# One shared PSUM bank for the small pieces of a graph-network kernel, and a new order of the tasks on every engine

## The chip, the cores and the metric

The kernel runs on one core of one Trainium2 chip. The metric is the device time of one execution in microseconds (us). The core's five engines work from queues of their own and meet only at semaphores: PE is TensorE (matmuls, with PEld for its weight loads), DVE is VectorE, ACT is ScalarE, POOL is GpSimd, and SP is SyncE, which only issues DMAs here. An instruction stands in its engine's queue in program order, so one that waits holds up all that stands behind it.

## The reference, cut to what matters

There are 32 graphs of 256 nodes with 64 features. For each node j of a graph the layer sums, over its neighbours k (the mask is set for about 5 of 256 nodes, itself included), a ReLU of a hidden vector of 192 values, and projects the sum back to 64:

```python
mask = (adj > 0.0).astype(x.dtype)
xj_proj = x @ W1a
diff = x[:, :, None, :] - x[:, None, :, :]
h = relu(xj_proj[:, :, None, :] + diff @ W1b + b1)
hm = einsum('bjkh,bjk->bjh', h, mask)
deg = sum(mask, axis=-1)
out = layernorm(x + hm @ W2 + deg[..., None] * b2)
```

The hidden vector of a pair (j, k) is u(j) + v(k) with u = x (W1a + W1b) + b1 and v = -x W1b. It is needed only where the mask is set.

## The kernel before, in words

**Two graphs at a time.** The 32 graphs make 16 pairs. A pair has TILES = 4 tiles of 128 nodes. The 192 hidden rows are split in a "main" part (128 rows, 4 groups of 128 columns) and a "tail" part (64 rows of each graph, put together in 2 groups).

**Slots and pieces.** The nodes are sorted by their number of neighbours (`sort_key`, `keys`, `ranks`, `permutation`), and each neighbour of a node gets a slot. Slot s is needed only for the first CAPS[s] nodes of the order. There are eleven pieces: 0, 1 and 2 cover all 128 nodes; pieces 3 to 9 cover 118, 96, 72, 48, 28, 16 and 10 nodes; piece 10 is the "small" piece, six slots of 6 nodes. For each piece `select` (DVE) makes a 0/1 matrix `hot` out of the slot numbers `slotT`, `seed` (ACT) copies u into a PSUM bank, `gather` (PE) adds hot times v on top of it (v in two float16 halves, `vh` and `vl`), and `add` (DVE, line 1737) takes the ReLU and adds it to `sums`. Main piece 0 goes another way: `take_out` (ACT) and `add_taken` (POOL, line 685). The small piece is clamped by `clamp_small` (ACT, line 897), reduced by `reduce_small` (DVE) and added by `add_small`, which ends the pair's sums (semaphore `summed`).

**Units and banks.** Pieces are grouped in units; a unit is one bank's worth, seeded and gathered together. Two ring buffers of two banks each serve all of it: one half of a buffer for tail units, the other for main units, so a unit can be seeded only when the unit two before it has been added (`released`).

**Stages of a pair.** `masks`, `count_masks`, `count_least`, `count_rest` (DVE) count neighbours; `turn_masks`, `number_slots` (PE) with `copy_maskT`, `copy_slots` (ACT) make the slots; `sort_x`, `excess_tail`, `hidden_u_main`, `hidden_u_tail`, `hidden_v` (PE) with `copy_xs`, `copy_u_main`, `copy_u_tail`, `high_v`, `full_v` (ACT) and `low_v` (POOL) make u and v; `start_sums` (DVE, line 1681, once a pair) starts `sums`; then come the pieces; `project` (PE) waits for `summed`, `copy_y`, `unsort_y`, `add_residual` (DVE, sets `z_added`), `statistics` (DVE), the moments, `scale` (POOL) and the store end the pair.

**Order.** Nothing schedules at run time. Each engine has a prologue written out by hand, a `body(pair)` that is run for 13 pairs by `run` (a hardware loop over six of them) and mixes the work of three to five neighbouring pairs, and an epilogue written out by hand.

**Scaling of the inputs.** Before the first v can be computed the weights are scaled by a power of two: `first_max` and `first_scales` do it for pair 0 from its own x. For all other pairs `sum_chunk` (ACT) sums the absolute values of the whole x in four chunks (`x_all`), `most`, `spread_x` and `scales` make the second factor.

## Time and profile before

| | before |
|---|---|
| median of 3 runs (lowest to highest) | 253.78 us (253.54 to 254.46) |
| span of the profiled execution, first to last instruction | 253.0 us |
| PE busy, share of the span | 239.2 us, 95% |
| DVE busy | 230.0 us, 91% |
| ACT busy | 214.8 us, 85% |
| POOL busy | 133.1 us, 53% |
| instructions PE, DVE, ACT, POOL | 2813, 810, 636, 288 |

The median stands 0.8 us above the profiled span; the profiled execution has no other time on record. A matmul's record is longer than its turn on the engine: in a run of equal matmuls the starts are closer together than the durations, so a busy PE says little about how much PE has to spare, and the distance from start to start is read instead. DVE's and ACT's records overlap their neighbours a little in the same way.

In rows of the view by windows the columns are: the window, its length, then busy us and count of PE, PEld, DVE, ACT and POOL, the granted PE clock (1.00 is full), the DMA share and GB/s. In rows of the view by groups they are: line, engine, operation, output<-inputs, shape, count, busy us, mean ns of one, and idle time of the engine before it. In rows of the timeline: start, duration, engine, line, operation, operands and how many were put together in the row.

### The profile page before, as it was taken

How to read it: one execution, taken by the hardware profiler on the slowest of the kernel's cores; microseconds unless marked ns; L12 is line 12 of the kernel's file. 1: busy time of each engine (PE TensorE's matmuls, PEld its weight loads, DVE VectorE, ACT ScalarE, POOL GpSimd, SP SyncE). 2: the span in 40 equal slices, each digit the busy share in tenths (PEclk: the TensorE clock that was granted, in tenths of full speed). 3: DMA queues.
4: the chain of work that ended last, by engine and by line, in shares of the span. 5: the costliest groups of instructions: out<-in, count | busy, mean ns of one | idle time of the engine just before them, and what ended most of it. 6: DMA issues, size and time to landing. Idle time of an engine off the chain costs nothing. (4 is left out here: it accounts for less than half of the span.)

```text
span 253.0 us, 9425 instructions
## 1 busy us (share of the span) xinstructions
PE 239.2 (95%) x2813; PEld 190.5 (75%) x2813; DVE 230.0 (91%) x810; ACT 214.8 (85%) x636; POOL 133.1 (53%) x288
## 2 busy tenths in 40 slices
PE   7968999999999999999999999999999999999990
PEld 2536687878887978878877878878887879777870
DVE  4797799999999999999999999999999999979853
ACT  2396999898989999898989989898989898988820
POOL 1415252565555574655554564655655555454834
PEclk9997999999999999999999999999999999999997
DMA  6992003501312203031212203031310110000001
GB/s 196 349 352 87 1 3 127 146 4 43 106 45 51 98 22 106 26 106 41 105 41 76 69 20 99 27 105 44 104 45 25 41 29 17 4 21 3 25 21 51
DMA packets 10552, 18.21 MB, mean 72 GB/s; under 512 B 1296, under 2 KB 7696, under 8 KB 10512
## 3 DMA queue, kind: packets, MB, share of 16 engines
q1 hardware_dynamic: 10512, 17.73, 21.7%
q8 instruction: 19, 0.31, 0.5%
q14 instruction: 21, 0.17, 0.2%
HBM read 15.63 MB, written 2.10 MB: 70 GB/s over the span
## 5 line engine op out<-in xcount | busy, mean ns | idle before, releaser
L1287 PE MATMUL ring<-hot,vh 128*128 128x128 bf16 (+9 forms) x768 | 115.8, 254 | 0.9 <-ACT ring L869 0.4
L1287 PE MATMUL ring<-hot,vl 128*128 128x128 bf16 (+9 forms) x768 | 113.9, 251 | 0.0
L1737 DVE SCALAR_TENSOR_TENSOR sums<-ring,sums 128x256 f32<-128x256 f32 (+14 forms) x304 | 104.9, 375 | 8.7 <-PE ring L1287 4.0
L1287 PEld LDWEIGHTS ring<-hot,vh 128*128 128x128 f16 (+1 forms) x768 | 61.0, 102 | 18.9 <-issue 7.9
L874 ACT COPY ring<-u_sb 128x144 f32<-128x144 f32 (+13 forms) x256 | 65.2, 302 | 9.6 <-DVE sums L1737 7.9
L1287 PEld LDWEIGHTS ring<-hot,vl 128*128 128x128 f16 (+1 forms) x768 | 62.2, 103 | 2.8
L631 POOL TENSOR_TENSOR vl<-vf,vh 128x384 f16<-128x384 f32 x32 | 34.4, 1075 | 49.2 <-ACT vf L839 32.3
L869 ACT COPY ring<-u_sb 128x512 f32<-128x512 f32 (+1 forms) x80 | 45.0, 565 | 0.9 <-PE ring L1111 0.4
L1710 DVE TENSOR_SCALAR hot<-slotT 128x944 bf16<-128x944 f16 (+6 forms) x112 | 28.5, 267 | 0.0
L685 POOL TENSOR_TENSOR sums<-taken,sums 128x512 f32<-128x512 f32 x16 | 20.3, 1272 | 11.7 <-ACT taken L891 11.7
L790 ACT CAST maskT<-bx 128x512 bf16<-128x512 f32 x32 | 18.4, 583 | 8.8 <-PE bx L1139 7.7
L797 ACT CAST slotT<-bx 128x512 f16<-128x512 f32 x32 | 19.0, 596 | 1.3 <-PE bx L1156 1.3
L1530 DVE TENSOR_REDUCE counts<-mask 128x8 f32<-128x1024 bf16 x16 | 19.1, 1195 | 0.0
L1257 PE MATMUL bx<-w2ms,sums 128*128 128x64 f32 x128 | 18.6, 268 | 0.0
L602 POOL TENSOR_TENSOR step<-stats 128x4 f32<-128x4 f32 x16 | 7.1, 441 | 21.1 <-DVE stats L1771 21.1
L839 ACT COPY vf<-bx 128x384 f32<-128x384 f32 x32 | 15.2, 477 | 3.5 <-PE bx L1225 3.4
L1257 PEld LDWEIGHTS bx<-w2ms,sums 128*128 128x128 f32 x128 | 16.9, 192 | 0.2
L1269 PE MATMUL bx<-y_sb,permT 128*128 128x64 f32 x128 | 16.2, 269 | 0.0
L832 ACT CAST vh<-bx 128x384 f16<-128x384 f32 x32 | 15.6, 487 | 0.3 <-PE bx L1225 0.3
L1269 PEld LDWEIGHTS bx<-y_sb,permT 128*128 128x128 f32 x128 | 15.5, 191 | 0.3 <-ACT y_sb L853 0.2
L1681 DVE SCALAR_TENSOR_TENSOR sums<-u_sb,bx 128x768 f32<-128x768 f32 x16 | 15.1, 945 | 0.1
L585 POOL TENSOR_TENSOR excess<-deg,given 128x4 bf16<-128x4 f32 x16 | 3.2, 203 | 22.0 <-DVE given L1606 22.0
(117 smaller groups left out, 470.8 us busy)
## 6 DMA issues: line engine op xcount, KB each, us to landing
adj_sb<-adj SPq DMA_DIRECT2D x16, 512.0 KB, 3.5
x_sb<-x_pairs SPq DMA_DIRECT2D x16, 128.0 KB, 2.3
xT_sb<-xT SPq DMA_DIRECT2D x16, 128.0 KB, 2.4
x_all<-x SPq DMA_DIRECT2D x4, 512.0 KB, 8.1
out<-o_sb SPq DMA_DIRECT2D x16, 128.0 KB, 1.7
wts<-weights SPq DMA_DIRECT2D x1, 417.0 KB, 4.8
cst_general<-general SPq DMA_DIRECT2D x1, 256.0 KB, 2.7
cst_half<-half SPq DMA_DIRECT2D x1, 137.0 KB, 3.2
```

The source lines that it names most:

```text
L631: eng.tensor_tensor(vl[pair.side][:, c, :], vf[:, c, :], vh[pair.side][:, c, :], ALU.subtract).then_inc(vl_ready, 1)
L685: eng.tensor_tensor(to, taken[piece][:, :, :], to, ALU.add).then_inc(taken_added, 1)
L790: eng.copy(maskT[:, g * NT:g * NT + NT, :].rearrange("p t r -> p (t r)"), (bx1, bx2)[g][:, :]).then_inc(maskT_copied, 1)
L797: eng.copy(slotT[:, g * NT:g * NT + NT, :].rearrange("p t r -> p (t r)"), (bx0, bx1)[g][:, :]).then_inc(slots_copied, 1)
L869: last = eng.copy(to, u.unsqueeze(1).broadcast_to([P, sum(map(whole, pieces)), n, P]))
L874: last = eng.copy(view(pair, part, unit, piece), v if slots == 1 else v.unsqueeze(3).broadcast_to([P, n, cap, slots]))
L1257: eng.matmul(to[:, g * O:g * O + O], sums[pair.side][:, NT + g * NT + t, :], w2ms[scaled(pair)][:, :], start=(g == 0), stop=False, skip_gr ...
L1269: last = eng.matmul(bx3[:, at:at + O], permT[pair.side][:, g * NT + t, :], y_sb[:, t * 2 + g, :], start=True, stop=True)
L1287: return eng.matmul(to if part == "main" else to[g * HT:g * HT + HT], values, selection, start=False, stop=final, skip_group_check=True)
L1530: eng.tensor_reduce(counts[pair.side][:, :, :].rearrange("p g c -> p (g c)"), mask[pair.side][:, :, :].rearrange("p c (k n) -> p (c k) n", ...
L1710: eng.tensor_scalar(to[:, :, :, off:off + n], slots, float(MARK + s), None, ALU.is_equal).then_inc(hot_ready, 1)
L1737: eng.scalar_tensor_tensor(out=to, in0=view(pair, part, unit, piece), scalar=0.0, in1=to, op0=ALU.max, op1=ALU.add).then_inc(added[part], 1)
```

## The change

Three things change. First, pieces are grouped in other units: piece 7 moves to the unit of piece 4, and the last unit is now pieces 8, 9 and 10 in both parts. Second, that last unit is "joint": its 6 groups x 62 columns of main and tail lie in one bank of the main half, seeded by one `seed_joint` for both parts, clamped by one `clamp_small`, and added by `add_joint` over all 6 groups; the tail half of the ring then turns over 3 units a pair and not 4. Third, the tasks stand in another order on all engines, and some gathers, `project` and `unsort_y` can be issued in parts (`first`, `end`) with other work between them. The load of pair 2's x also waits for `first_max` now.

```diff
-UNITS = {"tail": [[0, 1], [2, 3], [4, 5, 6], [7, 8, 9, 10]], "main": [[0], [1], [2], [3], [4], [5, 6], [7, 8, 9, 10]]}
+UNITS = {"tail": [[0, 1], [2, 3], [4, 7, 5, 6], [8, 9, 10]], "main": [[0], [1], [2], [3], [4, 7], [5, 6], [8, 9, 10]]}
...
+JOINT = {part: NU[part] - 1 for part in PART}
+RING_UNITS = {"tail": NU["tail"] - 1, "main": NU["main"]}
...
+                if not pair.general and isinstance(pair.n, int) and pair.n == 2:
+                    eng.wait_ge(x_max0_ready, 1)
...
+            def seed_joint(pair):
+
+                eng.wait_ge(u_copied["main"], pair.n + 1)
+                eng.wait_ge(u_copied["tail"], pair.n + 1)
+                released(pair, "main", JOINT["main"] - BUFFERS)
+                for piece in UNITS["main"][JOINT["main"]]:
+                    _, _, cap, slots = PIECES[piece]
+                    v = u_sb[pair.side][:, :, 0:cap]
+                    last = eng.copy(joint_view(pair, piece),
+                                    v if slots == 1 else v.unsqueeze(3).broadcast_to([P, GROUPS, cap, slots]))
+                last.then_inc(seeded["main"], 1)
...
-            def clamp_small(pair, part):
-                eng.wait_ge(gathered[part], NU[part] * (pair.n + 1))
+            def clamp_small(pair):
+                for part in PART:
+                    eng.wait_ge(gathered[part], NU[part] * (pair.n + 1))
...
+            def add_joint(pair, piece):
+
+                nth = JOINT_ADDS.index(piece)
+                if nth:
+                    eng.wait_ge(joint_added, len(JOINT_ADDS) * pair.n + nth)
+                else:
+                    for part in PART:
+                        eng.wait_ge(gathered[part], NU[part] * (pair.n + 1))
+                        eng.wait_ge(added[part], ADDS[part] * (pair.n + 1))
+                    eng.wait_ge(clamped, pair.n + 1)
+                to = sums[pair.side][:, :, 0:PIECES[piece][2]]
+                eng.scalar_tensor_tensor(out=to, in0=joint_view(pair, piece), scalar=0.0, in1=to,
+                                         op0=ALU.max, op1=ALU.add).then_inc(joint_added, 1)
```

A piece of DVE's new body; the other engines' orders are rewritten in the same way:

```diff
             def body(pair, has=always):
...
                 if has(-3):
+                    add_residual(elder)
+                if has(0):
+                    ranks(pair)
+                if has(-2):
+                    add(older, "main", 3)
+                if has(0):
+                    ranks_above(pair)
+                    permutation(pair)
+                if has(-1):
+                    start_sums(old)
```

**Where instructions move.** First VectorE's prologue, from the scaling of the first weights on. Before, the selection matrices of pair 0 follow it at once:

```order
L1650 TENSOR_SCALAR w1abs<-w1ab,up_bits 128x256
L1651 TENSOR_SCALAR w1vs<-wts,up_bits 128x192
L1698 TENSOR_SCALAR hot<-slotT 128x512 x2
L1522 TENSOR_SCALAR mask<-adj_sb 128x1024
L1610 CAST ident<-cst_half 128x128
L1701 TENSOR_TENSOR hot<-slotT,cst_half 128x512
L1530 TENSOR_REDUCE counts<-mask 128x8
```

The change has this ahead of the scaling (its lines have other numbers):

```order
L1675 SCALAR_TENSOR_TENSOR w_abs<-wts 64x192
L1583 TENSOR_SCALAR mask<-adj_sb 128x1024
L1591 TENSOR_REDUCE counts<-mask 128x8
L1667 TENSOR_REDUCE given<-above 128x4
L1607 TENSOR_TENSOR least<-counts,cst_single 128x8
L1689 TENSOR_REDUCE x_max<-x_sb 128x1
L1680 TENSOR_REDUCE w_top<-ring 128x1
```

and this from the last weight scaling on:

```order
L1712 TENSOR_SCALAR w1vs<-wts,up_bits 128x192
L1583 TENSOR_SCALAR mask<-adj_sb 128x1024
L1759 TENSOR_SCALAR hot<-slotT 128x512 x2
L1762 TENSOR_TENSOR hot<-slotT,cst_half 128x512
L1685 TENSOR_REDUCE x_most<-x_sum 128x1
L1771 TENSOR_SCALAR hot<-slotT 128x944
```

The mask and the counts of pair 1 moved ahead of the scaling, and the mask of pair 2 (the second `mask` row, right behind `w1vs`) moved ahead of pair 0's first selection matrix; the search of the largest x sum (`x_most`) moved into pair 0's selections.

Second, VectorE in the body, the end of a pair's adds, before (L1737 are the adds of single parts):

```order
L1737 SCALAR_TENSOR_TENSOR sums<-ring,sums 128x2x28
L1530 TENSOR_REDUCE counts<-mask 128x8
L1737 SCALAR_TENSOR_TENSOR sums<-ring,sums 128x2x16
L1737 SCALAR_TENSOR_TENSOR sums<-ring,sums 128x4x28
L1737 SCALAR_TENSOR_TENSOR sums<-ring,sums 128x2x10
L1737 SCALAR_TENSOR_TENSOR sums<-ring,sums 128x4x16
L1745 TENSOR_REDUCE small_sum<-small 128x36
L1737 SCALAR_TENSOR_TENSOR sums<-ring,sums 128x4x10
```

and of the change (L1810 is `add_joint`):

```order
L1796 SCALAR_TENSOR_TENSOR sums<-ring,sums 128x4x48
L1591 TENSOR_REDUCE counts<-mask 128x8
L1810 SCALAR_TENSOR_TENSOR sums<-ring,sums 128x6x16
L1796 SCALAR_TENSOR_TENSOR sums<-ring,sums 128x256
L1817 TENSOR_REDUCE small_sum<-small 128x36
L1810 SCALAR_TENSOR_TENSOR sums<-ring,sums 128x6x10
```

Four small adds (2x16, 4x16, 2x10, 4x10 columns) became two over six groups, and the adds of piece 7 (2x28, 4x28) moved up to those of piece 4.

Third, TensorE in its prologue around `spread_x` (the fp32 matmul from `x_most`), before:

```order
L1225 MATMUL bx<-w1vs,xT_sb 128x192 x4
L1111 MATMUL ring<-ones 128x512 x2
L1123 MATMUL bx<-reaches,cst_order 128x64 x3
L1139 MATMUL bx<-perm,mask 128x128 x8
L1100 MATMUL ring<-ident,x_most 128x128
```

and of the change:

```order
L1244 MATMUL bx<-xs,w1abs 128x256
L1132 MATMUL ring<-ident,x_most 128x128
L1257 MATMUL bx<-w1vs,xT_sb 128x192 x4
L1143 MATMUL ring<-ones 128x512 x2
L1155 MATMUL bx<-reaches,cst_order 128x64 x3
L1171 MATMUL bx<-perm,mask 128x128 x4
```

`spread_x` moved ahead of pair 0's `hidden_v` (the w1vs rows), so that v of pair 0 now stands behind a matmul that needs the sums over all of x.

## Rows read from the trace of the kernel before

**Rows 1.** The page's first part, busy time of the engines.

```profile
PE 239.2 (95%) x2813; PEld 190.5 (75%) x2813; DVE 230.0 (91%) x810; ACT 214.8 (85%) x636; POOL 133.1 (53%) x288
```

**Rows 2.** Windows cut at starts of start_sums of pairs 0, 1, 4, 8, 12, 15.

```profile
0.00:33.63 33.63, 27.56 (x224) 16.92 (x225) 25.05 (x79) 22.30 (x53) 10.64 (x24) 0.95 0.54 185
...
75.41:131.89 56.48, 56.02 (x693) 45.81 (x692) 55.07 (x197) 52.23 (x156) 32.94 (x69) 1.00 0.21 67
...
188.32:229.67 41.35, 40.90 (x510) 33.89 (x509) 38.28 (x137) 38.33 (x116) 22.75 (x50) 1.00 0.07 22
```

**Rows 3.** Timeline of TensorE, first and last row of one pair's turn.

```profile
119.97 0.39 PE L1237 MATMUL bx<-ident,perm 128*128 128x128 bf16 x4
...
134.10 0.39 PE L1237 MATMUL bx<-ident,perm 128*128 128x128 bf16 x4
```

**Rows 4.** Waits of VectorE and ScalarE: us in total, times, longest.

```profile
DVE sums L1737 <- PE ring L1287: 4.0, 13, 0.9
DVE sums L1737 <- POOL sums L685: 2.7, 2, 1.5
...
ACT ring L874 <- DVE sums L1737: 7.9, 19, 0.7
```

**Rows 5.** Groups by line and shape: VectorE's small adds.

```profile
L1737 DVE SCALAR_TENSOR_TENSOR sums<-ring,sums 128x96 f32<-128x96 f32 x16 | 4.1, 257 | 0.1
L1737 DVE SCALAR_TENSOR_TENSOR sums<-ring,sums 128x64 f32<-128x64 f32 x16 | 3.6, 224 | 0.0
L1737 DVE SCALAR_TENSOR_TENSOR sums<-ring,sums 128x40 f32<-128x40 f32 x16 | 3.1, 191 | 0.0
L1737 DVE SCALAR_TENSOR_TENSOR sums<-ring,sums 128x32 f32<-128x32 f32 x16 | 2.9, 181 | 0.1
L1737 DVE SCALAR_TENSOR_TENSOR sums<-ring,sums 128x20 f32<-128x20 f32 x16 | 2.7, 168 | 0.0
```

**Rows 6.** The load of pair 2's adjacency: its issue and time to landing.

```profile
L486 SPq DMA_DIRECT2D adj_sb<-adj x1: 652/652/652, 8.2 to 8.2; - x1
...
DMA to landing us min/median/max: 9.1/9.1/9.1
```

**Rows 7.** Timeline of VectorE in the prologue.

```profile
12.40 0.49 DVE L1698 TENSOR_SCALAR hot<-slotT 128x512 bf16<-128x512 f16 x2
12.81 0.69 DVE L1522 TENSOR_SCALAR mask<-adj_sb 128x1024 bf16<-128x1024 f32 x1
...
16.49 0.95 DVE L1681 SCALAR_TENSOR_TENSOR sums<-u_sb,bx 128x768 f32<-128x768 f32 x1
...
18.11 0.69 DVE L1589 TENSOR_TENSOR perm<-cst_half,rank 128x512 f32<-128x512 f16 x1
...
21.43 0.29 DVE L1659 TENSOR_REDUCE x_top<-ring 128x1 f32<-128x128 f32 x1 [0.65 <-PE ring L1100]
...
22.50 1.21 DVE L1530 TENSOR_REDUCE counts<-mask 128x8 f32<-128x1024 bf16 x1
...
33.63 0.95 DVE L1681 SCALAR_TENSOR_TENSOR sums<-u_sb,bx 128x768 f32<-128x768 f32 x1
```

**Rows 8.** A window behind TensorE's stops in the prologue.

```profile
21.20:24.20 3.00, 3.00 (x31) 2.72 (x31) 2.21 (x8) 1.31 (x3) 1.87 (x5) 0.50 0.53 183
```

**Rows 9.** Timelines of VectorE and TensorE at the last pair's end.

```profile
243.49 0.18 DVE L1753 TENSOR_TENSOR sums<-sums,small_sum 128x36 f32<-128x36 f32 x1
...
242.59 1.67 PE L1326 MATMUL bx<-ones 128*128 128x512 bf16 x7
244.10 0.55 PE L1257 MATMUL bx<-w2ms,sums 128*128 128x64 f32 x4
```

**Rows 10.** One source line each: durations in ns, min/median/max.

```profile
L1698 DVE TENSOR_SCALAR hot<-slotT x32: 279/285/741, 12.4 to 220.9; 128x512 bf16<-128x512 f16 x32
...
L631 POOL TENSOR_TENSOR vl<-vf,vh x32: 912/920/1357, 16.9 to 230.4; 128x384 f16<-128x384 f32 x32
```

More of the change, by code:

```diff
@@ new lines, in project, with unsort_y @@
+                if end == 3 * NT:
+                    last.then_inc(y_ready, 1)
+            def unsort_y(pair, first=0, end=TILES):
+                if first == 0:
+                    eng.wait_ge(y_copied, pair.n + 1)
+                    eng.wait_ge(permT_copied, pair.n + 1)
+                for c in range(first, end):
+                    g, t = divmod(c, NT)
+                    last = eng.matmul(bx3[:, (TILES + c) * O:(TILES + c + 1) * O], permT[pair.side][:, c, :],
+                                      y_sb[:, t * 2 + g, :], start=True, stop=True)
+                if end == TILES:
+                    last.then_inc(z_ready, 1)
@@ L1368, in body @@
                 if has(1):
-                    gather(new, "main", 4)
+                    gather(new, "main", 3, 2, 4)
                 if has(2):
@@ L1372, in body @@
                 if has(1):
-                    gather(new, "main", 5)
+                    gather(new, "tail", 2)
+                    gather(new, "main", 4, 0, 2)
                 if has(3):
@@ L1922, in _ @@
             run(eng, body)
+            select(Pair(0, 13), 6)
+            sort_key(Pair(0, 14))
+            add(Pair(0, 12), "main", 2)
+            add_residual(Pair(0, 11))
+            ranks(Pair(0, 14))
+            add(Pair(0, 12), "main", 3)
+            ranks_above(Pair(0, 14))
+            permutation(Pair(0, 14))
+            start_sums(Pair(0, 13))
+            add(Pair(0, 12), "tail", 4)
+            add(Pair(0, 12), "main", 4)
+            add(Pair(0, 12), "main", 7)
+            select(Pair(0, 13), 7)
```

792 lines of the change are left out of this document (398 added, 394 removed).

## The prediction

> **What bounds the kernel now.** I read the busy shares first. TensorE is at 95% and VectorE at 91% of the span [rows 1], but a matmul's record is longer than its turn, so the 95% doesn't say that TensorE is full. Next I cut the span at the starts of `start_sums`, which comes once a pair. The eight middle pairs take 14.12 us each (56.48 over four), the last three before the end 13.78, and the head up to the start of pair 1's sums 33.63 us [rows 2]. From there to pair 15's start at 229.67 are fourteen turns of 14.00 us on average. In a middle turn VectorE is busy for 55.07 / 4 = 13.77 us, so it idles for 0.35 us. ScalarE is busy for 13.06 and GpSimd for 8.2 us.
>
> For TensorE I read the starts: one turn goes from 119.97 to 134.10 [rows 3]. Between its first and last row I count a dozen places where the next start is later than the last form's own spacing; together these are about 1.06 us, so its own work is about 14.13 - 1.06 = 13.07 us. About seven of them, near 0.09 us each, stand where full-width matmuls follow half-width ones or the reverse, with every input long there. I take these 0.6 us as TensorE's own, which makes its line 13.65 to 13.7 us. Two engines within 0.5 us of the whole turn thus hold each other up. The list of waits says the same: VectorE's adds wait for gathers 13 times (4.0 us), the seeds wait for adds 19 times (7.9 us) [rows 4]. A gain has to shorten both lines, or take out waits between them.
>
> **What the change is worth in a middle turn.** *VectorE.* The adds of 32, 64, 20 and 40 columns take 181 + 224 + 168 + 191 = 764 ns. They become one of 96 columns (257 ns) and one of 60, which lies between 40 and 64 columns, 191 to 224; I take 215 ns [rows 5]. Records overlap their neighbours by about 80 ns, so two instructions fewer give back 2 x 80 less: 764 - 472 - 160 = 0.13 us a turn. VectorE can then turn in 13.77 - 0.13 = 13.64 us. *ScalarE* loses three copies and a clamp; it is busy for only 13.06 of 14.12 us [rows 2], so I cost this at nothing. If a seed were always late, this could give at most the 7.9 us that seeds wait now [rows 4], which are mostly its own idle time. *TensorE* keeps its 96 gather matmuls and their columns. In the new order the tail units stand together with `sort_x`, and I count five changes of width instead of seven, which is 0.18 us less: 13.5 us.
>
> So neither engine can turn in less than 13.5 to 13.65 us. Do the waits go? I laid the new bodies beside each other, with starts from the trace. The chain that comes nearest to closing starts at `project`: its product gives y, z, then `add_residual`; behind that VectorE has ranks, main 3, permutation, `start_sums`, tail 4, main 4 and main 7; then comes `seed_joint`, and only then main unit 6 on TensorE. The joint seed needs both adds of main 4 and 7 out of the bank. From `project` to main unit 6 this chain takes about as long as TensorE itself needs (9.25 us by my count from the starts), and 4.5 us more bring TensorE back to `project`: 13.75 us. I take 13.75 us, 0.37 less than 14.12. Twelve full turns and two shorter ones at the end (0.1 each) give 4.6; I allow 0.5 for turns before the new order has settled: **-4.1 us**. The bounds are the engine lines themselves, (14.00 - 13.5) x 14 = -7 us, and on the other side 0.15 us more waiting in each turn than now, +2 us.
>
> **The head.** Here I expect a loss. VectorE began pair 0's selections at 12.40 [rows 7]. Now the mask of pair 2 stands in front of them. Its adjacency was issued at 8.2 and landed 9.1 us later, at 17.3 [rows 6], and nothing in the change brings it sooner, since the loads ahead of it are the same. The mask's 0.6 us follow: the first selection at 18.0 instead of 12.40. Queued behind it are all selections of pair 0, `x_most`, and through that `spread_x`, behind which TensorE now has pair 0's `hidden_v`. From the first selection to `start_sums` were 4.1 us, with a mask of 0.6 and a count of 1.1 that are now done earlier: 2.4 remain. In front of `start_sums` come now also the second scaling (21.43 to 22.50, and its wait of 0.65 for TensorE) and pair 1's ranks and permutation, which stood behind it (from 17.36, where `start_sums` let go, to 18.7) [rows 7]: 1.7 + 1.3. Sum: 23.4 instead of 16.49.
>
> Most of this comes back, since the order ahead is then shorter. From the count at 22.50 to pair 1's `start_sums` at 33.63 were 11.13 us [rows 7], with waits of 0.9 and 1.5 in them [rows 4] and main 4 of 0.5 that now comes later: 8.2 us of work. In the new order that count stands about 1.5 us behind pair 0's `start_sums`, at 24.9. In front of the selections of pair 1 I expect a stop of about 1.9 us, since slot numbers need `turn_masks`, which stands behind `turn_perm`, which waits for `start_sums`; then two mask copies and four other copies are ahead of the second `copy_slots`. That puts pair 1's `start_sums` at 24.9 + 8.2 + 1.9 = 35.0. Add 0.8 for TensorE: after the stops in the old head the granted clock was 0.50, the 1.2 GHz level, from 21.20 to 24.20 [rows 8], and the new head lets TensorE idle longer (about 2 us up to `spread_x`, more up to pair 1's masks). 35.8 against 33.63: **+2.2 us**. If the stop is hidden and the clock stays up it is nothing, and it is +4 if the half clock lasts through pair 1.
>
> The Trainium skill (TensorE: Matmul & The Clock Gate, "What's actually happening") says that the gate's throttled state is the default and that activity releases it. The trace agrees with it here, with 0.50 behind the stops and 1.00 in the middle turns.
>
> **The end.** From 229.67 to the last add at 243.49 VectorE's work falls by two pairs' 0.13 us. Seven filler matmuls ran from 242.59 and `project` started at 244.10, 0.61 us after the last add [rows 9]; they now stand before main unit 1 of pair 15, where they can delay its gathers by 1.5 us that TensorE can spare less. I take 0.4 for the earlier `project` and 0.2 for the adds: **-0.6 us**, between -1.2 and +1.
>
> **Sum.** -4.1 + 2.2 - 0.6 = -2.5 us; the profiled span of 253.0 becomes 250.5. The median lies 0.8 above the span, so I forecast 251.3 us.
>
> **The rivals.** *The body gains and the head loses* is the forecast; with a turn of 13.65 to 13.85 us it gives 249.5 to 252.5. Chance 0.42.
>
> *The head costs nothing, or the turn gets near the engine lines.* For it: VectorE's wait for the adds taken out by GpSimd (2.7 us in two stops [rows 4]) lies in the head and in the end, and the new order has more work in front of main 1. The time is 251.3 - 2.2 = 249.1, or with a turn of 13.55 about 248.5. Chance 0.18.
>
> *VectorE's selections get shorter.* They take 279 ns at best and up to 741, and GpSimd's `low_v` 912 to 1357 [rows 10]: something holds both now and then. With two selections of this form in a turn, one slowed by 0.1 us, all of it is 0.1 x 14 = 1.4 us: 249.9, inside the first rival's time. Chance as a separate case 0.05. The Trainium skill (GPSIMD Engine Reference, "Key points") says that GpSimd shares its SBUF interfaces with VectorE, in contention with two-port modes and two SBUF inputs; the durations in rows 10 are of that kind, and no row shows the cause.
>
> *The joint bank is a new wait.* One seed now serves main and tail of the last unit. If main 4 and 7 are added 0.25 us later than I count, TensorE stops in front of main unit 6 in every turn, which turns in 14.0 us and more. At 14.12 nothing of the body's gain is left, and the head and end make it 253.8 + 2.2 - 0.6 = 255.4. It becomes slower than before by over 0.5% from a turn of about 14.1 on. For it: seeds already wait for adds 19 times. Against it: ScalarE has four instructions less. Chance 0.19.
>
> *No net change:* a turn near 13.95 loses to the head what the body gains; 252.6 to 254.9. Chance 0.16.
>
> **How the numbers follow.** About 0.5% (1.3 us) is what a measurement of this kernel can tell from no change. Faster than 252.5: most of the first case, both gains: 0.60. Within 0.5%: 0.19. Slower: 0.21. The range 248.3 to 255.0 leaves out the best and the worst corner, one in ten each; the likeliest case alone has 249.5 to 252.5.
>
> **What would show it.** In the trace after: pair 1's `start_sums` near 35.8 (the head is wrong below 34.5); VectorE idle just ahead of the mask at 17.3; middle turns of 13.65 to 13.85; no stop of TensorE over 0.1 us in front of the 124-column gathers; TensorE's clock at half somewhere between 19 and 27 us. The prediction is wrong if the middle turn is under 13.5, since then TensorE's width changes aren't its own time, or if pair 2's adjacency lands much before 17 us.

## The result and the profile after

The changed kernel takes 253.12 us (median of 16 runs, 252.27 to 254.37). The kernel before, run beside it, took 254.73 us (16 runs, 253.54 to 256.04); the ratio is 0.9938, with an interval of 0.9923 to 0.9954. So it is faster by 0.6%, about 1.6 us. I had forecast faster, by 2.5 us, to 251.3 us. In the whole study one execution was slow (one of run 2's ten, 300.87 us at a lower clock); no ratio contains it.

The busy shares of the page after the change, which stand against [rows 1]:

```profile
PE 235.9 (94%) x2810; PEld 188.7 (75%) x2813; DVE 226.6 (90%) x778; ACT 209.8 (84%) x572; POOL 121.4 (48%) x288
```

VectorE has 32 instructions fewer and ScalarE 64 fewer. Three windows answer to [rows 2]: the head up to pair 1's `start_sums`, four middle turns (pairs 4 to 8), and the end from pair 15's `start_sums`. The columns are length, then busy us (instructions) of PE, PEld, DVE, ACT, POOL, then clock, DMA share, GB/s.

```profile
0.00:36.72 36.72, 29.09 (x218) 17.13 (x219) 24.65 (x78) 22.05 (x50) 10.60 (x26) 0.86 0.49 170
77.95:132.49 54.54, 54.54 (x695) 45.36 (x692) 54.23 (x190) 50.88 (x142) 28.92 (x68) 1.00 0.23 69
...
227.03:250.90 23.87, 17.39 (x185) 13.49 (x183) 15.24 (x56) 11.05 (x35) 9.74 (x31) 0.97 0.06 20
```

Four turns now take 54.54 instead of 56.48 us, and TensorE and VectorE are busy for practically all of it. The head grew from 33.63 to 36.72, the end from 23.30 to 23.87. From pair 1 to pair 15 are (227.03 - 36.72) / 14 = 13.59 us a turn, against 14.00. In this pair of traces the change is therefore -5.7 us in the body, +3.1 in the head and +0.6 in the end, -2.1 together (253.0 to 250.9).

The timeline of VectorE in the new head, which stands against [rows 7]; the bracket is the idle time before a row and what ended it:

```profile
17.20 0.69 DVE L1583 TENSOR_SCALAR mask<-adj_sb 128x1024 bf16<-128x1024 f32 x1 [2.55 <-DMA adj_sb<-adj]
17.81 0.49 DVE L1759 TENSOR_SCALAR hot<-slotT 128x512 bf16<-128x512 f16 x2
...
23.77 0.94 DVE L1742 SCALAR_TENSOR_TENSOR sums<-u_sb,bx 128x768 f32<-128x768 f32 x1
```

The mask of pair 2 waits for its adjacency until 17.20, as forecast (17.3), the first selection starts at 17.81 instead of 12.40 (forecast 18.0), and `start_sums` at 23.77 (forecast 23.4). What lasts much longer than forecast is TensorE's half clock. These are four windows of the same trace, columns as above; the last but two is the granted clock, 0.50 being the 1.2 GHz level:

```profile
18.00:21.00 3.00, 2.25 (x10) 1.65 (x10) 2.56 (x15) 0.00 (x0) 0.00 (x0) 0.50 0.02 5
21.00:24.00 3.00, 1.50 (x9) 0.41 (x7) 2.05 (x11) 2.14 (x5) 1.47 (x2) 0.50 0.52 171
24.00:27.00 3.00, 2.75 (x24) 2.20 (x26) 2.83 (x6) 2.12 (x4) 3.00 (x9) 0.50 0.15 56
27.00:30.00 3.00, 3.00 (x44) 2.34 (x40) 0.89 (x4) 2.58 (x8) 0.66 (x2) 0.92 0.00 0
```

Before, only the stretch of [rows 8] was at 0.50. Now it is all of 18 to 27 (by narrower windows from about 17.2 to 27.5); between 15 and 18 TensorE was busy for 0.84 of 3 us.

The end, in rows of TensorE and then VectorE:

```profile
230.41 0.21 PE L1327 MATMUL ring<-hot,vh 128*128 128x124 bf16 x1 [1.05 <-ACT ring L914]
```

```profile
232.31 0.26 DVE L1810 SCALAR_TENSOR_TENSOR sums<-ring,sums 128x96 f32<-128x96 f32 x1 [1.55 <-ACT small L939]
...
242.63 0.19 DVE L1824 TENSOR_TENSOR sums<-sums,small_sum 128x36 f32<-128x36 f32 x1
```

From `start_sums` of pair 15 to the last add are now 15.60 us, against 229.67 to 243.49 = 13.82 in [rows 2, 9]. What follows the last add is shorter (8.3 instead of 9.5 us), since the filler no longer stands in front of `project` (run 3).

### The profile page after: what moved, and what is told of

It is laid out like the page before. It is cut to its first block and busy times, and to the rows that moved or that the text cites. A ratio compares the mean times of both kernels' runs of the same rounds, so it can differ in the third digit from the quotient of the medians.

```text
span 250.9 us, 9244 instructions
## 1 busy us (share of the span) xinstructions
PE 235.9 (94%) x2810; PEld 188.7 (75%) x2813; DVE 226.6 (90%) x778; ACT 209.8 (84%) x572; POOL 121.4 (48%) x288
## 5 line engine op out<-in xcount | busy, mean ns | idle before, releaser
L1327 PE MATMUL ring<-hot,vh 128*128 128x128 bf16 (+9 forms) x768 | 117.4, 255 | 1.3 <-ACT ring L914 1.0
L1327 PE MATMUL ring<-hot,vl 128*128 128x128 bf16 (+9 forms) x768 | 116.3, 251 | 0.0
L1796 DVE SCALAR_TENSOR_TENSOR sums<-ring,sums 128x256 f32<-128x256 f32 (+10 forms) x240 | 97.8, 428 | 4.3 <-PE ring L1327 1.9
L661 POOL TENSOR_TENSOR vl<-vf,vh 128x384 f16<-128x384 f32 x32 | 29.7, 929 | 63.2 <-ACT vf L870 59.4
L903 ACT COPY ring<-u_sb 128x192 f32<-128x192 f32 (+8 forms) x160 | 49.3, 359 | 7.4 <-DVE sums L1796 7.4
L900 ACT COPY ring<-u_sb 128x512 f32<-128x512 f32 (+1 forms) x80 | 43.3, 559 | 0.4 <-issue 0.2
L1304 PE MATMUL bx<-y_sb,permT 128*128 128x64 f32 x128 | 18.6, 272 | 0.0
L1188 PE MATMUL bx<-maskT,cst_half 128*128 128x128 bf16 x128 | 16.1, 221 | 0.1
L1583 DVE TENSOR_SCALAR mask<-adj_sb 128x1024 bf16<-128x1024 f32 x16 | 11.0, 688 | 5.4 <-DMA adj_sb<-adj 5.4
L1257 PE MATMUL bx<-w1vs,xT_sb 64*128 64x192 f32 x128 | 15.5, 362 | 0.3 <-ACT u_sb L855 0.3
```

The costliest lines, as they stand in the source:

```text
L661: eng.tensor_tensor(vl[pair.side][:, c, :], vf[:, c, :], vh[pair.side][:, c, :], ALU.subtract).then_inc(vl_ready, 1)
L900: last = eng.copy(to, u.unsqueeze(1).broadcast_to([P, sum(map(whole, pieces)), n, P]))
L903: last = eng.copy(view(pair, part, unit, piece), u[:, :, 0:PIECES[piece][2]])
L1304: last = eng.matmul(bx3[:, (TILES + c) * O:(TILES + c + 1) * O], permT[pair.side][:, c, :], y_sb[:, t * 2 + g, :], start=True, stop=True)
L1327: return eng.matmul(to if part == "main" else to[g * HT:g * HT + HT], values, selection, start=False, stop=final, skip_group_check=True)
L1796: eng.scalar_tensor_tensor(out=to, in0=view(pair, part, unit, piece), scalar=0.0, in1=to, op0=ALU.max, op1=ALU.add).then_inc(added[part], 1)
```

## The experiments

Head, turn and end below are read as above: the start of pair 1's `start_sums`, the mean turn from pair 1 to 15, and what follows pair 15's `start_sums`. A ratio is to the kernel before, run on the same chip. The kernels of runs 5, 6, 9, 10 and 13 to 18 leave a part of the work out, as each says; all of these but 10 are one execution each, so I compare their turns only. Four traces in which only the prologue or the end differs (after, 1, 2, 3) have turns of 13.58 to 13.59, so a difference of 0.02 us in one trace means nothing, and one of 0.05 does.

**1. The mask of pair 2 behind the scales.**

```
             first_scales()
-            masks(Pair(0, 2))
             select(Pair(0, 0), 0)
...
             scales()
+            masks(Pair(0, 2))
             count_rest(Pair(0, 1))
```

> The changed kernel with one row moved: the mask of pair 2 behind the second scaling instead of ahead of pair 0's selections. Theory 1 (the wait for pair 2's adjacency holds the head): the first selection starts when the slot numbers are there, near 15.9 us instead of 17.8, x_most follows at about 16.9 (the fourth chunk's sum), hidden_v at about 18.0 instead of 19.5, and pair 1's start_sums comes about 1.5 us earlier than 36.7. The time falls by 1.2 to 1.8 us against the changed kernel, ratio to the kernel before 0.988. Theory 2 (the sums over x stand ahead of u on ScalarE, and u is there only at 17.9, so the mask covers itself): the head ends where it did, within 0.4 us, ratio 0.993.

251.19 us, ratio 0.9864 (0.984 to 0.9887). The first selection starts at 15.71, now waiting for the slots and no longer for the adjacency; the head is 35.78, turn 13.58, end 23.86. The edit gives 0.9 us against the trace of after; against the mean head of after (below, 37.2) 1.4; by the two ratios, taken on two chips, 0.7%, 1.9 us. Theory 1 was right. The half clock did not go with the wait: it lasts from about 17.2 to 27.5 here too. This is the fastest version of the study that does all of the work.

**2. `spread_x` behind `hidden_v` as well.**

```
-            spread_x()
             hidden_v(Pair(0, 0))
+            spread_x()
```

> As the kernel with the late mask, and spread_x behind pair 0's hidden_v instead of ahead of it. Theory 1: hidden_v then waits for u alone (17.9 us); since x_most is there at about 17 anyway, this gives 0 to 0.5 us more than the late mask alone. Theory 2 (TensorE's slow clock after its stops prices the head, not the stops themselves): hidden_v keeps its 1.6 us at the half clock, and pair 1's start_sums moves by less than 0.3 us against the late mask alone.

255.61 us, ratio 1.002 (1.0004 to 1.0035). The head is 40.48, 4.7 us more than in run 1. `hidden_v` waits for u until 18.91, and `x_top` waits 2.65 us for `spread_x`, which now stands behind it; the half clock lasts from 19.3 to 33.0. Both theories missed: the new kernel's place for `spread_x`, ahead, is right.

**3. The filler matmuls back in front of the last `project`.**

```
             gather(Pair(0, 15), "main", 0)
-            keep_busy_last(7)
...
             add_over()
+            keep_busy_last(7)
             project(Pair(0, 15))
```

> The changed kernel with the seven filler matmuls again right ahead of the last project, and none ahead of main unit 1 of pair 15. Theory 1 (the filler ahead of main unit 1 delays project of pair 14 and the gathers of pair 15, on which VectorE waits 0.7 and 0.2 us): the last add comes 0.5 to 1.2 us earlier, the filler then costs 0 to 0.5 us at the end, net -0.3 to -0.9 us, ratio 0.991. Theory 2 (the end is set by the wait for the joint bank of pair 14, 1.55 us on VectorE, and the filler is covered by it): within 0.3 us of the changed kernel, ratio 0.993 to 0.995.

254.0 us, ratio 0.9966 (0.9946 to 0.9986). Head 36.16, end 24.76 instead of 23.87. From pair 15's `start_sums` to the last add are 15.61 us, as in after (15.60): where the filler stands now it costs nothing. Theory 2 had that much right; neither had the loss of 0.9 us at the end. Moving the filler gained 0.9 us; I had put it at 0.4, and the loss in the end lies elsewhere.

**4. The joint bank in the old order.** The new units and the joint seed, clamp and adds, with each body's tasks in the order of the kernel before (tail 3 right behind main 6, main 7 in front of main 5).

> The kernel before with the new units and the joint bank, in the old order: joint seed and clamp at the places of the main ones, tail unit 3 gathered right behind main unit 6, adds of piece 7 at the first place they can stand. Theory 1 (the body's gain of 0.5 us a turn comes from the instructions saved): a middle turn falls from 14.12 by 0.3 to 0.5 us, ratio 0.975 to 0.985, since the old head and end stay. Theory 2 (the gain comes from the order, the joint bank alone saves VectorE 0.13 us a turn or adds a wait): a middle turn of 14.0 to 14.3, ratio 0.992 to 1.015.

266.36 us, ratio 1.0445 (1.0426 to 1.0465); the turn is 14.71. Two rows of its list of waits:

```profile
ACT ring L913 <- DVE sums L1777: 30.8, 16, 2.4
PE ring L1326 <- ACT ring L913: 8.2, 16, 1.4
```

The joint seed waits 1.9 us in each turn for the add of main 7, and TensorE 0.5 us for the seed. This is the rival "the joint bank is a new wait": the mechanism is real, and dearer than I priced it (14.71 us a turn, where I had put 14.0 to 14.12). The order of the change takes it away. The end of this kernel, in the old order too, has 15.59 us from pair 15's `start_sums` to the last add, where before has 13.82.

**5, 6. Work taken from one engine.** `start_sums` on 384 of 768 columns; `hidden_v` on 96 of 192.

```
+                w = GROUPS * P if not pair.follows(2) else GROUPS * P // 2
...
+                        w = H // 2 if pair.follows(2) and not pair.general else H
```

> From pair 2 on, start_sums works on 384 instead of 768 columns, so the other half of the starting sums is left out (its values are then those of two pairs before); VectorE has about 0.45 us less work in each turn, nothing else changes. Theory 1 (VectorE alone sets the turn of 13.59 us: it was busy for 13.56 of 13.63 us in the middle turns): the turn falls by 0.35 to 0.45 us, to 13.15 to 13.25. Theory 2 (TensorE's own line of 13.5 us, with the width changes in it, stands right behind it, as the prediction had it): the turn falls by 0.05 to 0.15 us, to 13.45 to 13.55. Theory 3 (the chain from project over the joint seed sets it): start_sums is a link of that chain, so the turn falls as in theory 1, but then TensorE's waits for the joint seed get shorter, of which the trace shows none of length now.

> From pair 2 on, hidden_v computes 96 of 192 columns in each of its eight matmuls, so half of v is left as it was in the bank; TensorE has about 0.4 us less work in each turn, nothing else changes. Theory 1 (VectorE alone sets the turn): 13.55 to 13.60, as now, and TensorE idles 0.4 us more. Theory 2 (both lines stand side by side): the same within 0.05 us, since VectorE's 13.56 us remain. Theory 3 (TensorE alone sets the turn and VectorE is only full because it follows): 13.15 to 13.25. With the run before this one: if neither relief gives more than 0.15 us, the turn has two bounds; if one gives nearly all of its relief, that engine is the bound.

The turns are 13.56 and 13.55: neither engine's relief brings more than 0.04 us. In the second the eight matmuls of `hidden_v` took 0.62 instead of 0.85 us from start to next start, so the relief was 0.23, not 0.4. TensorE loses it again in front of `keys`, which writes a bank that ScalarE's copy of v (`full_v`) must have read. ScalarE's timeline and then TensorE's:

```profile
103.20 0.52 ACT L870 COPY vf<-bx 128x384 f32<-128x384 f32 x1
```

```profile
103.59 0.26 PE L1328 MATMUL ring<-hot,vl 128*128 128x236 bf16 x1
103.87 0.25 PE L1155 MATMUL bx<-reaches,cst_order 128*128 128x64 bf16 x3
```

In all eight middle turns `keys` starts 0.14 to 0.15 us behind the end of that copy, and 0.27 to 0.35 us behind the matmul ahead of it, where after has 0.10 to 0.12.

**7, 8. One more GpSimd operation, at two places.** The form is `low_v`'s, on data of its own.

```
                     degrees(second)
+                    work_beside()
...
                     add_taken(pair, 0)
+                if has(2):
+                    work_beside()
```

> GpSimd does one more operation of low_v's form (128x384, f32 and f16 in, f16 out, on data of its own) in each turn, behind degrees, where it idled for 1.8 us: beside VectorE's selections of 512 columns. Theory 1 (SBUF contention: the order of the change took the selections away from low_v, which is why the two selections of 512 columns took 588 ns a turn instead of 697): the selections become longer again, by 0.1 us or more in all, and as VectorE is full the turn grows by the same, 13.7 or more, 1.0065 or more in all. Theory 2 (the selections' length has another cause): selections of 290 ns as now, turn 13.59, no difference (within 0.2%).

> The same operation more for GpSimd, but behind add_taken, where it idled for 2.6 us in each turn: beside VectorE's adds of main 1, the mask and small operations. Theory 1 (contention with the SBUF-only selections alone): at most the mask (0.68 us) is slowed; turn 13.59 to 13.63, 1.000 to 1.003. Theory 2 (no contention, or any GpSimd work slows VectorE): no difference, or the same growth as beside the selections.

Beside the selections: 272.2 us, ratio 1.0704 (1.0671 to 1.0737), middle turn 15.16. Beside the adds: 258.5 us, 1.0169 (1.0126 to 1.0212), middle turn 14.00. GpSimd had been idle at both places. Its timeline and VectorE's in the first of the two:

```profile
103.57 0.92 POOL L751 TENSOR_TENSOR beside<-wts,beside_in 128x384 f16<-128x384 f32 x1
```

```profile
103.66 0.97 DVE L1768 TENSOR_SCALAR hot<-slotT 128x512 bf16<-128x512 f16 x1
...
104.66 0.28 DVE L1768 TENSOR_SCALAR hot<-slotT 128x512 bf16<-128x512 f16 x1
```

A selection of 0.28 us took 0.97: it began 0.09 us behind GpSimd's operation and ended 0.14 us after it (103.57 + 0.92 = 104.49). It wasn't slowed, it was held until the other was done. I summed, over eight middle turns, what each VectorE instruction took above the shortest of its form (where that is over 60 ns): 0.05 us a turn in the changed kernel, 1.66 with the operation beside the selections, 0.50 beside the adds. The turn grew by 1.56 and 0.40. So time held on a VectorE without slack goes into the turn nearly one to one. Run 7's theory 1 was right, and its price, 1.56 us a turn, far above the 0.1 that I had named as the least. Run 8's theories both missed: the mask wasn't held, but `least`, an operation of 8 columns with two inputs in SBUF, was, for 0.33 us a turn. The Trainium skill (Trainium Architecture — The Big Picture, "What this means for kernel authors") says that the port pair which VectorE and GpSimd share is an exclusive lock and not a split of bandwidth. The trace agrees: 0.97 us, and not 0.28 stretched in part.

**9. Both reliefs of 5 and 6 at once.**

> Both reliefs of the runs before in one kernel: from pair 2 on start_sums works on half its columns (-0.45 us of VectorE) and hidden_v on half its columns (-0.4 us of TensorE), so half of each result is left out. Alone neither moved the turn (13.53 to 13.57 us). Theory 1 (two lines of equal length, VectorE's and TensorE's, as the prediction had it): with both shorter the turn falls to 13.1 to 13.25. Theory 2 (a chain through several engines, in which neither operation stands, for instance mask, counts, sort key, ranks, slot numbers, or seed and add in turn, sets the turn): the turn stays at 13.5 or more.

Turn 13.52. Two lines of equal length in two engines, shortened by 0.45 and (as run 6 shows) 0.23, would have given about 13.35. TensorE stops in front of `keys` for ScalarE's copy as in run 6 (0.28 to 0.36 us between the starts): a third engine holds the turn.

**10. The kernel before, with `add_taken` on half its columns.**

```
-                to = sums[pair.side][:, PART["main"], :]
+                to = sums[pair.side][:, PART["main"], 0:P // 2]
```

> The kernel before with GpSimd's add_taken on half its columns (the other half of that one-hot part's contribution is left out), so that it takes about 0.7 instead of 1.27 us and ends before VectorE's first selection begins; VectorE's own instructions are all as they were. Theory 1 (the selection of 512 columns is held until GpSimd's operation beside it ends, 0.127 us a turn, and the change gained that part by its order): selections of 280 ns throughout, the turn falls from 14.00 to 13.85 to 13.90, ratio to before 0.990 to 0.994. Theory 2 (before is bound elsewhere and the held selection costs nothing there): selections short, turn 13.97 to 14.00, ratio within 0.2% of 1.

Ratio 0.9998 (0.9981 to 1.0015), turn 13.99. The selections were short (281 to 295 ns) in every turn, and nothing was gained. Theory 1 falls: in the kernel before 0.13 us a turn of selections was held, but not on the path that sets the turn. The result leaves out half of what `add_taken` adds.

**11. The joint bank in the old order, main 7 ahead of `start_sums`.**

```
                     add(old, "main", 4)
+                    add(old, "main", 7)
                 if has(0):
                     start_sums(pair)
                 if has(-1):
-                    add(old, "main", 7)
```

> The joint bank in the old order of tasks once more, with one add per turn moved: main 7, whose end the joint seed waits for, stands ahead of start_sums instead of behind it. Theory 1 (the loss of 0.75 us a turn came from start_sums, 0.95 us, standing in front of that add): the wait of the joint seed falls from 2.0 to 1.1 us a turn, and the turn from 14.75 to 14.0 to 14.1, ratio to before 1.000 to 1.010. Theory 2 (the joint seed is late whatever the adds do, since it also waits for the gather of tail 3 and the clamp, and the old order has them late): the turn stays above 14.5.

262.66 us, ratio 1.0318 (1.0295 to 1.0342), turn 14.48. The joint seed still waits 1.3 us a turn (14.1 us in 11 waits). The place of this add is a third of the loss, so neither theory's turn was met; the rest of the order is needed too.

**12. The first version, and pair 14's main 4 and 7 ahead of pair 15's `start_sums`.**

```
+            add(Pair(0, 14), "main", 4)
+            add(Pair(0, 14), "main", 7)
             start_sums(Pair(0, 15))
             add(Pair(0, 14), "tail", 4)
-            add(Pair(0, 14), "main", 4)
             add(Pair(0, 14), "tail", 7)
-            add(Pair(0, 14), "main", 7)
```

> The new kernel with pair 2's mask behind the scales (as in the first run) and, in the end, pair 14's adds of main 4 and 7 ahead of start_sums of pair 15 instead of behind it. Theory 1 (the end is longer than before because the joint seed of pair 14 waits 1.3 us for main 7, and TensorE 1.05 us for the seed): the stop of TensorE in front of the joint unit falls from 1.05 to under 0.3 us and the end part from 23.9 to about 23.1, ratio to before 0.983 to 0.984. Theory 2 (start_sums later by 0.6 us holds add_taken, main 1 and turn_perm, and what TensorE gains at the joint unit it loses there): end part 23.8 to 24.1, no difference to the first run.

252.2 us, ratio 0.9913 (0.9893 to 0.9932). TensorE's stop of 1.05 us at the joint unit is gone. In its place, in TensorE's timeline:

```profile
228.22 0.40 PE L1269 MATMUL bx<-ident,perm 128*128 128x128 bf16 x4 [1.23 <-DVE sums L1742]
```

`turn_perm` now waits 1.23 us for the later `start_sums`. From pair 14's `start_sums` to the end are 15.11 + 22.35 = 37.46 us, 0.6 more than in the first version, whose ratio of 0.9864 is the better one too. Theory 2 named the right place; it is a loss and not a draw.

**13 to 16. ScalarE relieved, and reliefs in the old kernel.** The four copies of v take half their columns (13, and 15 in the old kernel); 14 joins this to the reliefs of 5 and 6, and 16 is that of 5 in the old kernel:

```
+                n = 1 if pair.follows(2) and not pair.general else NT
```

> The new kernel; from pair 2 on ScalarE's four copies of v (vh and vf) take 192 of 384 columns each, so half of v is left as it was; ScalarE has about 0.12 us less in each, 0.48 us a turn. Theory 1 (ScalarE's line, 12.7 us of work and the stops that TensorE and VectorE give it, sets the turn; the prediction costed it at nothing): the turn falls from 13.59 to 13.1 to 13.3. Theory 2 (VectorE, at 13.56 us of work, takes over at once as in its own line): 13.50 to 13.58, no gain. Theory 3 (a chain in which only waits stand): 13.50 to 13.58 as well; the next run tells it from theory 2.

> The new kernel with all three reliefs (VectorE 0.45, TensorE 0.4, ScalarE 0.48 us a turn less, half of the starting sums, of hidden_v and of the copies of v left out). Theory 1 (each of the three engines has a line of about 13.5 us, so that only all together shorten it): the turn falls to 13.05 to 13.2. Theory 2 (VectorE and ScalarE only): the same here, and ScalarE's relief alone gives nothing. Theory 3 (a chain that none of the three is a link of): 13.4 to 13.55, and then the turn isn't set by the amount of work of an engine at all.

> The kernel before with the same relief of ScalarE (0.48 us a turn, about as much as the joint bank takes from it). Theory 1 (before is bound by ScalarE's line, and the change's three copies and a clamp fewer are where the gain of 0.4 us a turn comes from): the turn falls from 14.00 to 13.6 to 13.75. Theory 2 (the gain comes from the order, not from the work taken out): the turn stays at 13.9 to 14.0.

> The kernel before with start_sums on half its columns from pair 2 on (0.45 us of VectorE a turn less; the other half of the starting sums is left out). Theory 1 (VectorE was the bound before: 13.77 us of work in 14.12): the turn falls from 14.00 to 13.6 to 13.75. Theory 2 (it wasn't, since short selections gave nothing): the turn stays at 13.9 to 14.0.

ScalarE's relief in the new kernel gives nothing (13.59). All three together give 0.1 us (13.49). In the old kernel VectorE's relief gives 0.06 (13.94), and ScalarE's makes it slower: 14.30, with 14.7 to 15.0 in six of the turns. That last one is a hold again. VectorE's and GpSimd's timelines in it:

```profile
118.85 1.41 DVE L1591 TENSOR_TENSOR perm<-cst_half,rank 128x512 f32<-128x512 f16 x1
```

```profile
118.80 0.91 POOL L631 TENSOR_TENSOR vl<-vf,vh 128x384 f16<-128x384 f32 x1 [0.64 <-ACT vf L841]
```

With shorter copies `low_v` begins 0.05 us ahead of `permutation` and holds it: 1.41 instead of 0.69 us, and `turn_masks` on TensorE waits for it. Over eight middle turns `permutation` is held for 0.46 us a turn, and the turn is 0.44 longer (14.56 against 14.11). In the kernel before `low_v` began at 130.93 behind `permutation` at 130.81, and GpSimd was the one that was held: the 1357 ns of [rows 10].

All-relief left two stops in every turn, here on VectorE and on TensorE:

```profile
132.30 0.68 DVE L1800 SCALAR_TENSOR_TENSOR sums<-ring,sums 128x384 f32<-128x384 f32 x2 [0.41 <-PE ring L1330]
```

```profile
142.71 0.26 PE L1330 MATMUL ring<-hot,vl 128*128 128x236 bf16 x1
143.15 0.39 PE L1227 MATMUL bx<-perm,excess 128*128 128x128 bf16 x4 [0.18 <-DVE z L1836]
```

VectorE waits for the gather of main 5, then works without a stop over 0.1 us but one until `add_residual` reads the bank bx3; TensorE's `excess_main` waits for that, because it writes the same bank, and from it TensorE runs on to the gather of main 5. `start_sums` and `hidden_v` lie outside of both stretches. With ScalarE's copies shortened, `keys` has no stop any more (0.10 us), and the matmul ahead of `excess_main` has 0.33 to 0.47 us to the next start instead of 0.17 to 0.26.

**17, 18. Relief inside that chain.** Main 1 and 2 are added on half their columns, in the new and in the old kernel.

```
+                if part == "main" and piece in (1, 2) and pair.follows(2):
+                    to, of = to[:, :, 0:P // 2], of[:, :, 0:P // 2]
```

> The new kernel with VectorE's adds of main 1 and main 2 on half their columns from pair 2 on (256 of 512 each; the other half of these two contributions is left out): about 0.5 us of VectorE a turn less, as in the run with start_sums halved, but at another place, between the add of main 5 and add_residual. Theory 1 (a closed chain sets the turn: on VectorE from the add of main 5 to add_residual, about 10.7 us, and from there over excess_main and TensorE's gathers to main 5, about 2.8 us; start_sums and hidden_v are no links of it): the turn falls from 13.59 to 13.3 or less, down to where TensorE's own line holds (13.59 less its stops of 0.26 at excess_main and the masks). Theory 2 (the turn is set by something that VectorE's work has no part in): 13.5 to 13.55, as with start_sums halved.

> The same halved adds of main 1 and main 2 in the kernel before (half of two contributions left out). There VectorE waits 0.33 us for the gather of main 2, and TensorE 0.2 us in front of excess_main; between the two stand main 2, two selections, a mask, main 3, tail 3 and add_residual on VectorE. Theory 1 (the chain of before runs about 11 us on TensorE, from excess_main to the gather of main 2, and 3.2 us on VectorE): one of the two halved adds is a link, so the turn falls from 14.00 by about 0.2 us, to 13.75 to 13.85. Theory 2 (no such chain): 13.9 to 14.0, as with start_sums halved.

New kernel: turn 13.56. Old kernel: 13.91, 0.09 less, which is theory 2's time; what bounds the old kernel's turn stays open. In the new one, the windows of the same stretch as above and VectorE's stop:

```profile
77.95:132.49 54.54, 54.54 (x694) 45.46 (x696) 52.22 (x189) 50.40 (x141) 30.14 (x68) 1.00 0.22 68
```

```profile
144.94 0.42 DVE L1835 TENSOR_TENSOR z<-bx,xb 128x256 f32<-128x256 f32 x1 [0.41 <-PE bx L1304]
```

VectorE has 0.5 us a turn less to do (52.22 instead of 54.23 over four) and now waits for TensorE's `unsort_y`, while TensorE is busy throughout as before. From start to next start its groups of matmuls take the same as in the changed kernel, within 0.02 us a turn. I had expected 13.3, with TensorE's stops gone; they weren't stops but its own time.

## Why the prediction came out as it did

The bounds of the turn were read rightly. The steps that failed are the turn of 13.75 us, the work and the half clock in the head, the end, and the 0.8 us between span and median.

**What bounds the kernel after: as forecast, with the figures moved.** TensorE's own line, its pauses at changes of width included, is 13.56 to 13.58 us (run 17: VectorE relieved where it matters, TensorE unchanged), where I had 13.5. Less work on VectorE or ScalarE alone gives 0.00 to 0.04 us (runs 5, 13, 17). Right behind this line stand two chains through other engines. With TensorE relieved (runs 6 and 9) the turn stayed at 13.55 and 13.52 and TensorE stopped at `keys`, for ScalarE's copy of v; with those copies shortened too (run 14) it stayed at 13.49 and TensorE stopped at `excess_main`, for VectorE's stretch from main 5 to `add_residual`. So bounds do stand side by side, and ScalarE, which I had costed at nothing, is in one of them. That the turn falls when all three are relieved inside these chains wasn't run.

**The body, -5.7 us instead of -4.1.** The step that failed is "I take 13.75 us": a chain from `project` over `add_residual`, main 4 and 7 and the joint seed to main unit 6. It is there (run 4 shows it at 14.7 when the order doesn't serve it), but in the new order it has slack; the turn goes down to TensorE's line. Middle turns are 0.51 us shorter (56.48 against 54.54 over four, and 13.60 over the eight), not 0.37: over twelve full turns 1.7 us, the whole miss of this term. The 0.5 us for turns in which the order settles were right: those after pairs 1 and 2 took 13.94 and 13.72. The 0.13 us for VectorE's adds (764 - 472 - 160) held over these four turns: its busy time fell from 55.07 / 4 = 13.77 to 54.23 / 4 = 13.56, and of these 0.21 some 0.08 are time held by GpSimd (before 0.13 us a turn in selections, after 0.05 in `least`). Over the eight turns it fell by 0.29, which leaves 0.21. The joint adds took 254 and 215 ns where I had 257 and 215.

**Where the gain is on TensorE.** From start to next start, over eight middle turns: the gathers 7.33 to 7.08 us a turn, `turn_masks` 0.61 to 0.46, `hidden_u` 1.26 to 1.12, all else +0.03 together; sum 14.11 to 13.60. I put this down to fewer changes of width and fewer waits for seeds, the permutation and xs, without a run that parts them. The edit's first part, the shared bank, gives none of it alone (run 4, +0.7 us a turn); it is the order that pays, and I can't say how much of it the bank lets it save, since the new order with separate banks wasn't run.

**The head, +3.1 us instead of +2.2.** The place and the cause were right to within 0.5 us up to `start_sums` of pair 0 (23.77 for 23.4). Two steps behind it failed. The first is the work itself: from there to the count are 1.86 us where I had 1.5, and from the count to pair 1's `start_sums` 11.09, of which 2.55 are stops (I had 1.9 and the 0.8) and 8.5 work (I had 8.2). The second is "Add 0.8 for TensorE": the half clock lasts from 17.2 to 27.5 us and not for some 3 us, and when it ends varies. Ten traces with the changed kernel's head (after and runs 3, 5 to 9, 13, 14, 17) have pair 1's `start_sums` at 36.12 to 37.90, mean 37.2; five with the old head (before, 10, 15, 16, 18) at 33.05 to 34.18, mean 33.6. So the head's true price is nearer +3.7. The time from pair 0's to pair 1's `start_sums`, which I had at 12.4, follows the end of the half clock:

| end of the half clock behind pair 0's `start_sums` | from pair 0's to pair 1's `start_sums` | traces |
|---|---|---|
| 3.5 to 3.8 us | 12.83 to 13.01 us | after, 3, 12, 14 |
| 4.6 to 5.1 | 13.37 to 13.44 | 1, 7, 17 |
| 5.9 | 13.75 | 8 |
| 6.4 to 6.6 | 14.02 to 14.11 | 2, 5, 6, 9, 13 |

The old head shows the same: in four traces the half clock ends 7.6 to 7.9 us behind pair 0's `start_sums` and this time is 17.12 to 17.14; in run 16 it ends 10.6 us behind and the time is 18.17. Which of TensorE's stops brings the half clock on so early in the new head stays open: run 1 took the 2.55 us wait for the mask away, and the level still fell at 17.2. Run 6 has the latest, 37.90, and there the clock is still down in the last of the four windows:

```profile
27.00:30.00 3.00, 3.00 (x30) 2.56 (x28) 0.42 (x1) 2.14 (x6) 0.47 (x1) 0.50 0.00 0
```

The Trainium skill (TensorE: Matmul & The Clock Gate, "What's actually happening") has the throttled state as the default that activity releases; the trace of after agrees with it: the level fell at 17.2, in a stretch in which TensorE was busy for 0.84 of 3 us, stayed down over one with 1.50 (21 to 24), and came back at 27.5, behind one with 2.75.

**The end, +0.6 us instead of -0.6.** The step that failed is "I take 0.4 for the earlier `project` and 0.2 for the adds". The filler's move gained 0.9 (run 3), but the adds, taken as 0.2 shorter, are 1.8 longer (15.60 against 13.82 from `start_sums` to the last add). The joint bank, which is harmless in the middle, brings stops of 1.05 us on TensorE and 1.55 on VectorE there. The joint bank in the old order has the same 15.59 (run 4), and 14.89 with main 7 earlier (run 11), so the bank brings this in the old order as well. That nothing else covers the clamp and the seed there is my reading. I had looked for this wait in the body alone.

**The sum.** With the mean heads it is -5.7 + 3.7 + 0.6 = -1.4 us, near the 1.6 of the ratio. The forecast of -2.5 came that near by luck: a gain of the body that was 1.6 too small stood against a head and an end that were together 2.7 too cheap. Of the absolute miss, 253.12 against 251.3 us, most is another step: "The median lies 0.8 above the span". That figure set the median of three executions against the span of a profiled one whose own time wasn't on record. In every execution for which both are on record the time is 1.7 to 1.9 us above the execution's own span (after: 252.74 and 250.9). The miss of 1.8 us is 0.4 in the span (250.9 for 250.5), 1.0 in this step, and 0.4 by which the profiled execution was faster than the median.

**The rivals.** "The joint bank is a new wait" is true of the bank, and in this order of the end alone. "VectorE's selections get shorter" came true in the trace (349 to 294 ns on average over the middle turns) and was worth nothing in the kernel before, as run 10 shows. "The turn gets near the engine lines" came true in the body (13.60 us, where I had named 13.55), together with a head that cost more.

## What to carry to other kernels

An order tuned so that no stop is left anywhere still has a bound; to find it, take work out at several places and look which stop opens. A relief that gives nothing says that its place is off the chain, or that another chain is as long, and not that its engine has room. Before two engines' tasks are moved, look which GpSimd operation will run beside which SBUF-only operation of VectorE: the one that starts second waits for nearly all of the first, and 0.05 us decided who it was in run 15. Price a prologue with the matmul clock in it: the same head took 12.8 to 14.1 us for one pair by when the clock came back, so it takes several traces to measure. Price the last turns apart from the middle ones. And set a time against a span of the same execution only.

## What the runs showed of the hardware

In five traces (before, after, 7, 8, 15) I took every VectorE instruction that began while a GpSimd operation of over 0.5 us was running and ran 0.15 us or more on. Held were selections (f16 to bf16 in SBUF; of 512 columns 26 of 38, up to 0.77 us above the shortest) and operations with two inputs in SBUF: `permutation` (median 0.74 us, where GpSimd had 0.87 left to run), `add_small` (0.74 at 0.87), and even `least` with 8 columns (up to 0.78). In all 86 held cases the time lost is what GpSimd's operation still had to run less 0.11 to 0.13 us. Not held were the adds that read PSUM (111 of 256 columns: 0.03 us at most, where GpSimd had 0.66 left in the median), the count over the mask (0.03 at most) and `statistics` (0.03 at most). The Trainium skill (GPSIMD Engine Reference, "Specifications") names VectorE's two-port modes and two SBUF inputs as what contends, and the trace agrees for two SBUF inputs; in which mode a selection runs no trace here shows. Of the selections of 944 columns 6 of 26 were held, up to 1.08 us. The other 20 all began beside a GpSimd operation that itself took over 0.06 us more than its shortest, so there it was GpSimd that had been held.

So less work on ScalarE could make the old kernel 0.3 us a turn slower (run 15). TensorE stops for about 0.1 us (0.09 to 0.10) at each change between gathers of full and of half output width with all inputs long there, in before, after and runs 4, 11 and 17 alike; those pauses are part of its line.
